# Input weights in four contiguous parts, the identity on ScalarE's queue, three small vectors in one load

## What is computed

```python
# x: (2, 1024, 512) f32; W_in (1024, 512), W_out (512, 1024); I = 1536
def attn(x, W_in, b_in, W_out, b_out, gamma, beta):
    u = einsum('bsd,hd->bsh', x, W_in) + b_in
    def step(state, u_t):
        s = tanh(u_t + state * gamma + beta)      # 1024 steps, one behind the other
        return s, s
    states = scan(step, zeros, u over s)
    return einsum('bsh,dh->bsd', states, W_out) + b_out
def ffn(x, gate_w, up_w, down_w, ...):            # weights rounded to float8_e4m3fn
    fuse = silu(x @ q(gate_w) * gate_scale) * (x @ q(up_w) * up_scale)
    return (fuse @ q(down_w)) * down_scale
x = x + layernorm(attn(layernorm(x), ...))
x = x + layernorm(ffn(layernorm(x), ...))
```

## Time and profile before

| what | value |
|---|---|
| median of 3 runs | 557.77 us (557.42 to 558.75) |
| the profiled execution's own time | 557.68 us |
| its span | 555.9 us |
| granted TensorE clock, mean | 0.997 |
| PE busy | 537.8 us, 97% |
| DVE busy | 446.1 us, 80% |
| ACT busy | 374.8 us, 67% |

### The profile page before, as it was taken

One profiled execution on the slowest core, in us unless ns is written; L12 is line 12 of the kernel. 1 busy time (PEld: TensorE's weight loads), 2 busy tenths in 40 slices (PEclk: granted clock), 3 DMA queues, 4 the chain that ended last, 5 costly groups with the idle time before them and its releaser, 6 DMA issues.

```text
span 555.9 us, 11947 instructions
## 1 busy us (share of the span) xinstructions
PE 537.8 (97%) x2958; PEld 456.6 (82%) x2958; DVE 446.1 (80%) x2608; ACT 374.8 (67%) x2317; POOL 247.6 (45%) x372
## 2 busy tenths in 40 slices
PE   7999989899998999999999999999999999999995
PEld 5875768788788788889889888988888888899994
DVE  3699999888797998888897888778987988885414
ACT  2677695865678677877788667876677767662332
POOL 1213454857449343653248243562351343635532
PEclk9999999999999999999999999999999999999998
DMA  8886789973104200130003000300002000100011
GB/s 262 254 265 191 152 200 227 182 171 57 48 15 150 59 2 2 38 97 2 1 2 113 21 1 2 106 11 2 1 2 77 1 2 1 64 16 1 1 39 38
DMA packets 25333, 39.92 MB, mean 72 GB/s; under 512 B 3760, under 2 KB 8496, under 8 KB 25264
## 3 DMA queue, kind: packets, MB, share of 16 engines
q1 hardware_dynamic: 19904, 30.24, 17.0%
q0 software_dynamic: 4608, 8.39, 8.8%
q10 hardware_dynamic: 752, 0.54, 0.3%
HBM read 26.57 MB, written 4.20 MB: 55 GB/s over the span
## 4 chain that ended last, share of the span: by engine, by line
PE 64%; DVE 6%; ACT 2%; issue 0%; POOLq 0%; DVEq 0%; POOL 0%; ACTq 0%
PE gate_up L1130 26%; PE wide L1086 15%; PE wide L1160 13%; PE wide L1055 10%; DVE recur L1230 2%; ACT pairs L1555 1%; DVE recur_second L1230 1%; PE wide L1106 1%; ACT pairs L1540 1%; DVE fused L1363 1%; DVE z L1376 0%; DVE stats_z L1244 0%; DVE x_lo L1345 0%; ACT gated L1590 0%; DVE x_res L1303 0%
## 5 line engine op out<-in xcount | busy, mean ns | idle before, releaser
L1555 ACT ACTIVATE pairs<-recur 128x8 f32<-128x8 f32 x768 | 137.3, 179 | 89.8 <-DVE recur L1230 89.8
L1230 DVE TENSOR_TENSOR_SCAN recur<-recur,pairs 128x16 f32<-128x16 f32 x768 | 150.9, 196 | 49.5 <-ACT pairs L1555 46.8
L1555 ACT ACTIVATE pairs<-recur_second 128x8 f32<-128x8 f32 x768 | 136.7, 178 | 0.0
L1230 DVE TENSOR_TENSOR_SCAN recur_second<-recur_second,pairs 128x16 f32<-128x16 f32 x768 | 133.0, 173 | 0.0
L1753 POOL TENSOR_TENSOR fused_lo<-fused,fused_hi 128x256 fp32r<-128x256 f32 x95 | 70.4, 742 | 128.7 <-ACT fused_hi L1608 128.4
L1086 PE MATMUL wide<-w_out_sb,pairs 128*128 128x512 f32 (+1 forms) x272 | 112.1, 562 | 0.9 <-ACT pairs L1562 0.5
L1055 PE MATMUL wide<-x_norm_t,w_in_sb 128*128 128x256 f32 x448 | 101.9, 380 | 0.9 <-DVE y L1280 0.9
L1086 PEld LDWEIGHTS wide<-w_out_sb,pairs 128*128 128x128 f32 x272 | 75.5, 298 | 26.5 <-ACT pairs L1564 0.8
L1055 PEld LDWEIGHTS wide<-x_norm_t,w_in_sb 128*128 128x128 f32 x448 | 83.7, 190 | 13.1 <-DVE y L1280 1.2
L1160 PE MATMUL wide<-down_q,fused_hi 128*128 128x512 f32 x192 | 82.6, 430 | 0.3 <-POOL fused_lo L1753 0.3
L1590 ACT ACTIVATE gated<-gate_up,gate_scale_cols 128x128 f32<-128x128 f32 (+1 forms) x169 | 63.4, 378 | 26.2 <-PE gate_up L1130 26.1
(11 more groups left out here) (135 smaller groups left out, 795.5 us busy)
## 6 DMA issues: line engine op xcount, KB each, us to landing
x_res<-x SPq DMA_DIRECT2D x16, 256.0 KB, 3.3
x_in<-x SPq DMA_DIRECT2D x14, 256.0 KB, 4.3
out<-z SPq DMA_DIRECT2D x14, 256.0 KB, 2.5
x_norm_t<-x_t SPq DMA_DIRECT2D x5, 512.0 KB, 3.5
raw_own<-rounders POOLq DMA_DIRECT2D x9, 256.0 KB, 5.0
w_in_sb<-w_in_t SPq DMA_DIRECT2D x4, 512.0 KB, 7.5
w_out_sb<-w_out_t SPq DMA_DIRECT2D x8, 256.0 KB, 4.6
raw_own<-down_w SPq DMA_DIRECT2D x8, 256.0 KB, 4.8
```

The lines of the kernel that those rows point to most:

```text
L1230: eng.tensor_tensor_scan(preact_of[b].rearrange("p c k -> p (c k)"), factors_of[b].rearrange("p c k -> p (c k)"), pairs[:, t % RING, colum ...
L1555: ins = eng.activation(pairs[:, t % RING + 1, columns, 0], preact_of[b][:, :, 1], ACT.Tanh)
```

## The change

The host lays `w_in` out as four arrays of 128 partitions by 1024 values, so that part m is one contiguous row of 4 KB for each partition, both in memory and in the tile `w_in_sb`; before, a part was four pieces of 1 KB for each partition. The products read the same 128 x 128 blocks, at other places of the tile. The load of the identity goes from SP's list (between x and `w_in`) to ACT's list (behind ACT's two loads of x, ahead of the first activation). `b_in`, `beta` and `gamma` come as one array of 128 x 24 values in one load, and DVE's wait for them is for one load instead of three.

```diff
-        w_in_sb = sb("w_in_sb", [P, KD, hidden])
+        w_in_sb = sb("w_in_sb", [P, MS, KD, 2 * P])
...
                     eng.dma_start(x_in[0:P:batch, g, :], x_blocks[0][0][:, g, :]).then_inc(s_first_x_in[g], 16)
-                eng.dma_start(ident[:, :], identity).then_inc(s_ident_in, 16)
                 for m in range(MS):
                     yield HEAD + 1 + m
-                    ms = slice(2 * m * P, 2 * (m + 1) * P)
-                    eng.dma_start(w_in_sb[:, :, ms], w_in_t[:, ms].rearrange("(k p) h -> p k h", p=P)
+                    eng.dma_start(w_in_sb[:, m, :, :].rearrange("p k h -> p (k h)"), w_in_parts[m, :, :]
                                   ).then_inc(s_w_in_in[m], 16)
...
                             ins = eng.matmul(first_u_bank(j),
-                                             w_in_sb[:, k, j * P:(j + 1) * P], x_norm_t[:, k, 0:P],
+                                             w_in_sb[:, j // 2, k, j % 2 * P:(j % 2 + 1) * P], x_norm_t[:, k, 0:P],
...
-                eng.wait_ge(s_small_in, 48)
+                eng.wait_ge(s_small_in, 16)
...
                     eng.dma_start(x_in[1:P:batch, g, :], x_blocks[0][1][:, g, :]).then_inc(s_first_x_in[g], 16)
+                eng.dma_start(ident[:, :], identity).then_inc(s_ident_in, 16)
                 yield HEAD + 0.5
-                eng.dma_start(cols[:, 0, :], b_in).then_inc(s_small_in, 16)
-                eng.dma_start(cols[:, 1, :], beta).then_inc(s_small_in, 16)
-                eng.dma_start(cols[:, 2, :], gamma).then_inc(s_small_in, 16)
+                eng.dma_start(cols[:, :, :].rearrange("p v j -> p (v j)"), u_columns).then_inc(s_small_in, 16)
```

More of the change, by code:

```diff
@@ L519, with recurrent_sandwich_kernel @@
          "first_u": (26, 28, 30, 32), "first_u_copy": (31, 33, 35, 37)}
-def recurrent_sandwich_kernel(nc, x, x_t, w_in_t, w_out_t, b_in, beta, gamma, b_out, gate_w, up_w, down_w,
+def recurrent_sandwich_kernel(nc, x, x_t, w_in_parts, w_out_t, u_columns, b_out, gate_w, up_w, down_w,
                               gate_scale, up_scale, down_scale, identity, out):
     batch, seq, dim = x.shape
-    hidden = w_in_t.shape[1]
+    hidden = w_out_t.shape[0]
     inner = gate_w.shape[1]
@@ L1027, in project_first_u @@
                             ins = eng.matmul(wide[quad][:, jj * P:(jj + 1) * P],
-                                             w_in_sb[:, k, j * P:(j + 1) * P], x_norm_t[:, k, P:2 * P],
+                                             w_in_sb[:, j // 2, k, j % 2 * P:(j % 2 + 1) * P], x_norm_t[:, k, P:2 * P],
                                              start=(k == 0), stop=(k == KD - 1))
@@ L1055, in project_u @@
                                 ins = eng.matmul(wide[bank][:, jj * TOK:(jj + 1) * TOK],
-                                                 w_in_sb[:, k, j * P:(j + 1) * P], x_norm_t[:, k, :],
+                                                 w_in_sb[:, j // 2, k, j % 2 * P:(j % 2 + 1) * P], x_norm_t[:, k, :],
                                                  start=(k == 0), stop=(k == KD - 1))
@@ L1798 @@
         "x_t": a["L0_attn_x"].transpose(2, 1, 0).reshape(a["L0_attn_x"].shape[2], -1),
-        "w_in_t": a["L0_attn_W_in"].T,
+        "w_in_parts": a["L0_attn_W_in"].T.reshape(-1, P, a["L0_attn_W_in"].shape[0] // (2 * P), 2 * P).transpose(2, 1, 0, 3).reshape(
+            a["L0_attn_W_in"].shape[0] // (2 * P), P, -1),
         "w_out_t": a["L0_attn_W_out"].T,
-        "b_in": columns(a["L0_attn_b_in"]),
-        "beta": columns(a["L0_attn_beta"]),
-        "gamma": columns(a["L0_attn_gamma"]),
+        "u_columns": _np.concatenate([columns(a["L0_attn_" + name]) for name in ("b_in", "beta", "gamma")], axis=1),
         "b_out": a["L0_attn_b_out"].reshape(1, -1),
```

## The result

| | before | after |
|---|---|---|
| median of 7 runs | 557.77 us (557.08 to 558.86) | 561.65 us (559.24 to 563.81) |
| ratio | | 1.0068, interval 1.0052 to 1.0085 |
| profiled execution, span | 557.68, 555.9 us | 563.81, 562.0 us |
| scan of step 0 starts | 17.10 us | 21.79 us |
| granted TensorE clock, mean | 0.997 | 0.988 |

The change makes the kernel 3.9 us slower, 0.7%. The forecast was 0.9 us faster, and even the rival on the slow side stopped at 558.3. The profiled execution is the slowest of its seven; its 6.1 us of longer span are worked out here, and the spread is taken up further on. The kernel before was executed again beside each group of experiments, and their ratios are against those executions. Two of its 23 in the last group took 916 us at a granted clock of 0.56, which nothing here explains, and the ratios leave them out.

What follows compares the result with a forecast made beforehand. The start of step 0's scan at 17.10 us was taken to pace the recurrence, PE's long stretch and the end. 1.04 us won at group 0 less 0.15 for the identity gave 0.9 us, so 556.8 us, range 555.8 to 558.3.

Steps and rivals of the forecast that it cites:

- the rival on the slow side: In the head: the identity takes gamma's 5.6 us, lands at 7.9, transposes start 1.6 us late; 558.3 us, chance 0.08.
- What bounds the kernel: Whole kernel: the recurrence and PE's long stretch hang on scan 0's start at 17.10 us; a microsecond saved there moves the end.
- Part (c): Identity on ACT's queue: issued 0.3 us later, landing at 6.5 us, 0.15 us lost; bounds no cost to 1.6 us.
- The second rival: In the head: identity rows alternate with 4 KB w_in rows, landing at 7.3 us; gain gone, 557.7 us, chance 0.13.
- the sum: Head to end: 1.04 us won at group 0, 0.15 lost by the identity, 0.9 us faster: 556.8 us.
- Part (b): w_in in 4 KB rows: part 0 lands early enough for PE's first input products to start 1.04 us earlier.
- The first rival: In the head: long rows don't speed the stream, part 0 lands at 8.0, 0.6 us won; 557.1 us, chance 0.14.
- Part (a): SP's queue: without the identity ahead, the first w_in load is issued at 1.98 instead of 2.61 us, 0.63 us earlier.
- (d): One load of the three vectors: issued near 2.9 us, lands between 7.1 and 8.5 us; no gain and no loss.
- (e): SP's later issues move up by 0.6 us or more; the first raw weight keeps 1.9 us of slack before scan 0.

Runs made afterwards that it cites:

- (7): The changed kernel executed once more, unaltered, for a second look at the head: 560.00 us, one execution.
- experiment 1: The changed kernel with the identity issued on SP's queue again, ahead of the input weights; long rows and single vector load kept: 557.77 us, ratio 0.9998.
- (2): The kernel before with nothing but the long rows of w_in; identity on SP, three small vector loads: 557.28 us, ratio 0.9994.
- (5): The changed kernel with the identity one place further forward on ACT's queue, ahead of its load for tile 1 of x: 556.99 us, ratio 0.9992.
- experiment 6: The changed kernel with five products on zeros instead of three: 559.19 us, ratio to the kernel before 1.0026.
- (8): The kernel before with three products put into TensorE's gap near 170 us: 557.14 us, ratio 0.9987; the same products were also put into three other kernels.
- experiment 4: The changed kernel, but SP issues the input weights only after the identity has landed: 558.93 us, one execution.
- experiment 3: The kernel before with nothing but the identity moved to ACT's queue, w_in in 1 KB rows: 559.18 us, ratio 1.0035; a second profile took 559.59 us.

## Why the prediction was wrong

**What bounds the kernel: right.** The end follows scan 0 as claimed. In every profile, the span less the start of scan 0, less 1.7 us where the clock fell near 170 us, is the same within 0.8 us, while scan 0 moves by 6.0; the six profiles that the table leaves out give 538.6 to 539.1:

| kernel | scan 0 | span | difference | fall near 170 us | without it |
|---|---|---|---|---|---|
| before | 17.10 | 555.9 | 538.8 | no | 538.8 |
| after | 21.79 | 562.0 | 540.2 | yes | 538.5 |
| after, second execution (7) | 19.31 | 558.2 | 538.9 | no | 538.9 |
| identity on SP (1) | 16.43 | 557.4 | 541.0 | yes | 539.3 |
| rows alone (2) | 15.97 | 555.3 | 539.3 | no | 539.3 |
| identity one place forward (5) | 15.75 | 554.7 | 539.0 | no | 539.0 |
| five products on zeros (6) | 18.00 | 557.2 | 539.2 | no | 539.2 |
| before, gap filled (8) | 16.05 | 554.9 | 538.9 | no | 538.9 |

**Part (c), the price of the identity: the step that failed.** I put it at 0.15 us from the row of `b_in` and bounded it at 1.6 us by the slowest small load of that queue. Both rows came from a kernel in which `w_in` was issued later and in shorter rows, and the same change moved `w_in` forward and lengthened its rows. Both were also loads of 4 KB, a sixteenth of the identity. The bound was taken from rows that the change itself alters. The landing was 7.3 us after the issue (6.2 to 6.5 in three other profiles), outside the bound of 5.6. Without `w_in` beside it the identity takes 2.9 us, so the company of 4 KB rows costs 3.3 to 4.4, and that of 1 KB rows 2.1 to 2.9. The second rival was nearest in mechanism, one row of the identity between two of `w_in`, and had too small a price, 1.4 us on top of the identity's 3.6. It counted the identity's own rows alone. In the four profiles with 4 KB rows these took 1.8 to 2.9 us longer than in experiment 4, and they also started 0.4 to 1.7 us later, behind rows of x that `w_in` had held up in the same way. The Trainium skill names the mechanism, engines that go round between the queues packet by packet ("DMA: Bandwidth & Descriptors", Queues, rings and completion order). The trace agrees that two queues share the engines (2.9 us alone, 5.0 to 7.3 us beside `w_in`) and that the identity's eight rows at an engine don't go as one: of its 128 packets 116 have another that starts 21 to 26 ns behind them in experiment 4, and 18 in experiment 6. A strict alternation isn't shown, since the trace doesn't give the engine of a packet, and in the other three profiles with 4 KB rows more of them follow each other (62 to 86).

**The missing term: TensorE's clock.** No part of the sum and no rival asked what PE's idle time would do to it. For the profiled execution this term is the largest, 2.3 us in the head's products, some 0.5 in the transposes and 1.7 near 176 us. "TensorE: Matmul & The Clock Gate" (What's actually happening), a page of the Trainium skill, says that the array falls to half clock when it has been idle. The trace agrees: 3.18 us of waiting were followed by the 0.50 level, the products on zeros, which stand there to prevent this, having ended at 6.4 us. Seen from there, an input of the first transpose that is late was the one thing that the head could not afford.

**Part (b), the long rows: direction right, size within noise.** Part 0 landed 5.3, 4.8 and 5.1 us after its issue with long rows and the identity on SP. But the kernel before with the gap filled, whose head is unchanged, had 4.9, where its first profile had 6.0; there the 1 KB rows ran at 333 GB/s from 5 to 6 us, where rows 8 have 191, and the long rows of experiments 1 and 2 at 365 and 357. Even in the first profile the engines were full two microseconds before the 9 us of the prediction, with 338 GB/s and a DMA share of 1.09 from 7 to 8 us. I took a single landing and a single rate for constants, and by this second profile most of the 1.04 us that I hoped to win were one unlucky draw of the old kernel. The first rival, that long rows don't speed the stream, is nearer to what the runs show. In the kernel after itself part 0 took 7.3 us: the queues disturb each other in both directions.

**Part (a), (d) and (e): right in effect.** The first `w_in` load was issued at 1.99 us. The joined load landed at 10.8 us, later than the 8.5 I gave, and DVE waited 0.74 us for it, but ACT's first copy of u came at 15.0. The first raw weight landed at 14.0, with scan 0 at 21.8.

**The sum.** For the median the chance of "slower by more than 0.3%" was set at 0.06, because I let only a landing past 9 us get there. With the clock the point lies much nearer: in the second profile of experiment 3, 559.6 us were reached with the identity at 8.1.

## What to carry to other kernels

Before an early small load is moved to another queue, ask what the large loads on the first queue will look like after the whole change, not before it; a load that gates the first instruction of TensorE belongs ahead of the bulk in time, whichever queue it stands on (one place further forward was enough). The loads that stand ahead of it in its own queue count as well: here they were held up in the same way. An idle stretch on TensorE has two prices, the wait and the half clock behind it, and the second can be as large as the first. A time of landing in one profile is one draw: here it varied by a microsecond between executions of the same head, as much as the edit could win.

## What the runs showed of the hardware

A gap of only 1.75 to 1.83 us in TensorE's products, with continuous work for over 5 us on either side, was followed by the 1.2 GHz level in three profiled executions (the kernel after at 176 us, experiment 1 at 172 us, experiment 4 at 171 us) and not in seven others (the kernel before, experiments 2, 5, 6 and 7, and both of experiment 3). It cost 1.7 us each time, and this fits the two clusters of times of a kernel that does the same work. Three products of 1.46 us in all, put into the gap, removed the upper cluster: 16 of 29 runs lay above 558.0 us without them, and none of 12 with them. What decides between the executions was not measured.

Rows of two queues share the 16 DMA engines in small portions. The identity, 128 rows of 512 bytes on ACT's queue, landed 2.9 us after its issue with only x beside it, 5.0 and 5.8 us after it beside 1 KB rows on SP's queue, and 6.2 to 7.3 us after it beside 4 KB rows.
